# Feed-forward of a tree-routed audio block: ACT weighs four of eight levels, GpSimd adds the residual, and the four groups of an overflow tile are added up in one PSUM bank

## What is computed

```python
for _ in range(DEPTH + 1):                      # 8 levels of a binary tree with 255 nodes
    score = einsum('td,td->t', x, w1s[current]) + b1s[current]
    choice = ((sign(score) + 1) / 2)
    current = current * 2 + choice + 1
path_weights = gelu(abs(logits), approximate=False)       # (2992 tokens, 8)
for i in range(DEPTH + 1):
    t_i = einsum('td,tdo->to', x, w2s[nodes_i]) + b2s[nodes_i]    # a 64x64 matrix of the token's own node
    out = out + t_i * path_weights[:, i][:, None]
return h + out
```

## Time and profile before

| | us |
|---|---|
| median of 3 runs | 495.93 (495.58 to 497.63) |
| the profiled execution, its own time | 497.14 |
| its span (first to last instruction) | 495.4 |
| from the first product of the feed-forward (365.07) to the span's end | 130.3 |

### The profile page before, as it was taken

How to read it: one execution, slowest core, us unless ns; L and a number is a source line. 1 busy time by engine, 2 the same in 40 slices (tenths; PEclk the granted TensorE clock), 3 DMA queues, 4 the chain that set the end, 5 groups by cost and what they waited for, 6 DMA issues and landing times.

```text
span 495.4 us, 8210 instructions
## 1 busy us (share of the span) xinstructions
PE 362.6 (73%) x2578; PEld 246.1 (50%) x2578; DVE 353.8 (71%) x619; ACT 297.0 (60%) x691; POOL 266.6 (54%) x354
## 2 busy tenths in 40 slices
PE   1158997767998897878987798834069887778880
PEld 1145665545555554456644475522057665545550
DVE  0558869897988888988889979776129999433341
ACT  1357987799789986777976658561013332544551
POOL 4324687885686846855896617417506555321111
PEclk9988989999999999898998989855569999999997
DMA  4443541339969722312441200197151220000000
GB/s 95 120 104 84 125 101 41 93 78 226 202 146 156 162 53 63 93 33 63 110 109 27 69 1 11 38 133 99 32 132 35 56 54 10 6 7 4 7 3 7
DMA packets 58424, 36.99 MB, mean 75 GB/s; under 512 B 31645, under 2 KB 57079, under 8 KB 58378
## 3 DMA queue, kind: packets, MB, share of 16 engines
q1 hardware_dynamic: 54250, 33.55, 33.6%
q0 software_dynamic: 3328, 2.36, 1.9%
q10 hardware_dynamic: 800, 0.49, 0.5%
HBM read 11.15 MB, written 7.50 MB: 38 GB/s over the span
## 4 chain that ended last, share of the span: by engine, by line
DVE 39%; PE 27%; ACT 15%; issue 11%; DMA 5%; POOL 1%; SPq 1%; DVEq 0%; POOLq 0%; ACTq 0%
DVE nm L1367 12%; ACT Z L1183 8%; PE Z L914 8%; DVE pre L1634 6%; PE Z L1051 5%; DVE va L1626 4%; DMA pre<-in_x 3%; DVE va L1396 2%; PE Z L1053 2%; ACT q L1125 2%; PE Z L1057 2%; DVE pre L1463 1%; ACT k L1125 1%; ACT va L1276 1%; PE Z L1055 1%
## 5 line engine op out<-in xcount | busy, mean ns | idle before, releaser
L1367 DVE TENSOR_REDUCE nm<-Z 125x1 f32<-125x748 f32 x192 | 175.4, 932 | 38.9 <-PE Z L914 33.2
L1183 ACT ACTIVATE Z<-Z,nm 125x748 f32<-125x748 f32 x192 | 166.1, 870 | 61.5 <-DVE nm L1367 61.2
L914 PE MATMUL Z<-pool_a 128*125 128x512 f16 (+1 forms) x768 | 164.5, 342 | 27.3 <-ACT Z L1183 23.7
L914 PEld LDWEIGHTS Z<-pool_a 128*125 128x125 f16 x768 | 88.7, 141 | 71.6 <-ACT Z L1183 45.6
L717 POOL DMA_INDIRECT out<-pre,va x44 | 42.7, 971 | 87.8 <-DVE pre L1640 78.3
L1634 DVE TENSOR_REDUCE pre<-va 128x64 f32<-128x512 f32 x44 | 45.1, 1025 | 1.3
L1276 ACT COPY va<-Z 32x520 f32<-32x520 f32 x48 | 27.9, 580 | 30.3 <-PE Z L1057 30.1
L781 PE MATMUL Z<-xhT,wq 128*128 128x249 f16 (+1 forms) x192 | 33.4, 295 | 10.5 <-DVEq L1377 9.2
L1183 ACT ACTIVATION_READ_ACCUMULATOR Z<-Z,nm 125x1 f32 x192 | 41.1, 214 | 0.0
L1051 PE MATMUL Z<-pool_a,qk 128*32 x96 | 29.6, 390 | 14.1 <-ACT va L1276 8.7
L646 POOL DMA_INDIRECT sorted_rows<-xrow,slot x24 | 30.4, 1266 | 15.3 <-DVE slot L1519 8.7
(11 more groups left out here) (237 smaller groups left out, 620.9 us busy)
## 6 DMA issues: line engine op xcount, KB each, us to landing
pool_a<-pool_a SPq DMA_DIRECT2D x64, 187.0 KB, 3.3
pool_a<-pool_a SPq DMA_DIRECT2D x64, 93.5 KB, 2.2
sorted_rows<-zrow SPq DMA_DIRECT2D x1, 3640.0 KB, 22.1
va<-sorted_rows SPq DMA_DIRECT2D x11, 260.0 KB, 3.4
w<-in_L_ffn_w2s SPq DMA_DIRECT2D x1, 2048.0 KB, 16.6
pre<-in_x SPq DMA_DIRECT2D x4, 375.0 KB
pool_a<-in_L_ffn_w2s SPq DMA_DIRECT2D x1, 1024.0 KB
out<-pre,va POOLq DMA_INDIRECT x44, 2.1
```

Of the source, the lines that this page charges most:

```text
L914: last = mm(z[0:XP, c0:c1], kst[:, u % 3, a, hd, KST[t]:KST[t] + XP], qst[:, u % 3, hd, c0:c1], start=(a == 0), stop=(a == 1))
L1183: sc_.activation(z, z, ACT.Exp, bias=nm[0:XP, u % 4, i:i + 1], accum_out=sm[0:XP, u % 4, i:i + 1]).then_inc(s_exp, 1)
L1367: v.tensor_reduce(nm[0:XP, u % 4, i:i + 1], Z[n % 3][0:XP, 0:N], X, ALU.max, negate=True).then_inc(s_max, 1)
```

## The change

Four edits in the feed-forward:

1. ACT weighs the first four levels of each tile (`weigh_first`: four ACTIVATE of 128x64 from PSUM, scaled by a column of `gw`), DVE the other four.
2. GpSimd adds the residual in `rows_out`, ahead of the tile's output DMA; `add_residual` is gone.
3. An overflow tile uses one bank pair like a static one. Each group is multiplied with all 128 columns of weights, 32 of them with the group's rows and 96 zero, and the four groups are added up in the bank. For that ACT spreads the transposed rows in `xm`, where each group's 32 columns stand between blocks of zeros that are written once (`apart_zeros`). The four copies to `yv` are gone.
4. The leaves of four groups lie in one number (`lam4`, two more DVE operations before `group_offsets`). PE loads one number for a tile, after group 0 of the tile before; each node is `(leaves >> (7 * g + sh)) & mask`. The load for a block's first tile now stands ahead of the block's `If`.

```diff
             def rows_out(k):
+                pool.wait_ge(s_sl, k + 1)
+                o = yo[:, k % NO, :]
+                gp.tensor_tensor(o, o, xs[:, (k // 4) % NX, k % 4, C_H:C_ID], ALU.add).then_inc(s_yo, 1)
                 pool.wait_ge(s_yo, k + 1)
...
             def bank_ready(n):
-                if n >= ST_TILES + NY:
-                    pe.wait_ge(s_yv, n - NY - ST_TILES + 1)
-                elif n >= NY:
+                if n >= NY:
                     pe.wait_ge(s_wy, n - NY + 1)
+                    pe.wait_ge(s_wa, n - NY + 1)
...
                 def node(g, sh):
-                    if g % 2:
-                        return pairs[g // 2] >> (7 + sh)
-                    return (pairs[g // 2] >> sh) & (LEAVES - 1 >> sh)
+                    return (leaves >> (7 * g + sh)) & (LEAVES - 1 >> sh)
                 tile_ready(k)
-                xk = xsT[:, k // 4 % 3, (k % 4) * P:(k % 4 + 1) * P]
+                bank_ready(k)
+                y = y_bank(k)
                 for g in range(4):
-                    if g == 2 and k % 4 < 3:
-                        following = load_leaves(k + 1)
-                    bank_ready(banks(k) + g)
-                    y = Z[1 + (banks(k) + g) % NY][0:G, :]
-                    xg = xk[:, G * g:G * (g + 1)]
-                    mm(y[:, 0:4 * E1], xg, wlow[:, bass.ds(node(g, 4) * (4 * E1) + T03 * E1, 4 * E1)], start=True, stop=True)
+                    xg = xm[:, k // 4 % 2, k % 4, P * g:P * (g + 1)]
+                    f, l = g == 0, g == 3
+                    mm(y[:, 0], xg, wlow[:, bass.ds(node(g, 4) * (4 * E1) + T03 * E1, 4 * E1)], start=f, stop=l)
...                                                        (three more products, alike)
+                    if g == 0 and k % 4 < 3:
+                        following = load_leaves(k + 1)
...
             for m in range(ST_TILES // 4, F_TILES // 4):
+                leaves = load_leaves(4 * m)
                 with pe.If(groups > 4 * (4 * m - ST_TILES)):
                     xs_T(m)
-                    pairs = load_leaves(4 * m)
...
+            def weigh_first(k):
+                act.wait_ge(s_gelu, k + 1)
+                if k >= 2:
+                    act.wait_ge(s_sl, k - 1)
+                y = y_bank(k)
+                for n in range(AW):                                  # AW = 4
+                    last = sc_.activation(wy[:, k % 2, n * D:(n + 1) * D], y[:, 0, n, 0:D], ACT.Copy,
+                                          scale=gw[:, k % 4, n:n + 1])
+                last.then_inc(s_wa, 1)
...
                     for k in range(4 * m, 4 * m + 4):
-                        if k >= ST_TILES + 2:
-                            act.wait_ge(s_wy, k - 1)
-                        for g in range(4):
-                            act.wait_ge(s_y, banks(k) + g + 1)
-                            sc_.copy(yv[g * G:(g + 1) * G, k % 2], y_bank(banks(k) + g)[0:G]).then_inc(s_yv, 1)
-                        act.wait_ge(s_yv, 4 * (k - ST_TILES + 1))
-                        gates(k, yv[:, k % 2])
+                        gates(k)
+                        weigh_first(k)
...
             def weigh(k):
-                v.tensor_tensor(wy[:, k % 2].rearrange("p (h l o) -> p h l o", h=2, o=D), y[:, :, :, 0:D],
-                                gw[:, k % 4].rearrange(...).to_broadcast([P, 2, 4, D]), ALU.mult).then_inc(s_wy, 1)
+                v.tensor_tensor(w[:, 1], y[:, 1, :, 0:D], gv[:, 1], ALU.mult).then_inc(s_wy, 1)
             def sum_levels(k):
                 dve.wait_ge(s_wy, k + 1)
+                dve.wait_ge(s_wa, k + 1)
```

More of the change, by code:

```diff
@@ L1029, in load_leaves, with overflow_products @@
                 kk = k - ST_TILES
-                return [nc.tensor.value_load(lami[0:1, 2 * kk + i:2 * kk + i + 1], min_val=0,
-                                             max_val=LEAVES * LEAVES - 1) for i in range(2)]
-            def overflow_products(k, pairs):
+                return nc.tensor.value_load(lam4[0:1, kk:kk + 1], min_val=0, max_val=LEAVES ** 4 - 1)
+            def overflow_products(k, leaves):
                 following = None
                 def node(g, sh):
-                    if g % 2:
-                        return pairs[g // 2] >> (7 + sh)
-                    return (pairs[g // 2] >> sh) & (LEAVES - 1 >> sh)
+                    return (leaves >> (7 * g + sh)) & (LEAVES - 1 >> sh)
@@ L1059, in overflow_products @@
+                last.then_inc(s_y, 1)
                 return following
@@ L1242, in _, with apart_zeros @@
             sc_.activation(warm[:], half[0:1, 0:1], ACT.Gelu)
+            def apart_zeros():
+                act.wait_ge(*freed["sl", B - 1])
+                n = 8 * 4 * (P + G)
+                sc_.copy(pre[:, NO * D:NO * D + n], zrow[:, 0:1].to_broadcast([P, n])).then_inc(s_xmz, 1)
             def xs_copy(m):
@@ L1246, in xs_copy, with xs_copy_apart, gates @@
                 if m >= 3:
-                    act.wait_ge(s_y, banks(4 * (m - 2)))
+                    act.wait_ge(s_y, 4 * (m - 2))
                 sc_.copy(xsT[0:D + 1, m % 3, :], Z[0][0:D + 1, 512 * (m % 2):512 * (m % 2) + 512]).then_inc(s_xc, 1)
-            def gates(k, y):
+            def xs_copy_apart(m):
+                act.wait_ge(s_xp, m + 1)
+                if m >= ST_TILES // 4 + 2:
+                    act.wait_ge(s_y, 4 * (m - 1))
+                sc_.copy(xm[0:D + 1, m % 2].rearrange("p t (g c) -> p t g c", c=P + G)[:, :, :, 0:G],
+                         Z[0][0:D + 1, 512 * (m % 2):512 * (m % 2) + 512].rearrange(
+                             "p (t g c) -> p t g c", t=4, g=4)).then_inc(s_xc, 1)
+            def gates(k):
+                act.wait_ge(s_y, k + 1)
                 if k >= 4:
                     act.wait_ge(s_wy, k - 3)
+                y = y_bank(k)
                 w = gw[:, k % 4].rearrange("p (h l) -> p h l", h=2)
@@ L1262, in _ @@
                     xs_copy(k // 4 + 1)
-                act.wait_ge(s_y, k + 1)
-                gates(k, y_bank(k))
+                gates(k)
+                weigh_first(k)
             act.wait_ge(s_goff, 1)
@@ L1268, in _ @@
                 with act.If(groups > 4 * (4 * m - ST_TILES)):
-                    xs_copy(m)
+                    xs_copy_apart(m)
                     for k in range(4 * m, 4 * m + 4):
-                        if k >= ST_TILES + 2:
-                            act.wait_ge(s_wy, k - 1)
-                        for g in range(4):
-                            act.wait_ge(s_y, banks(k) + g + 1)
-                            sc_.copy(yv[g * G:(g + 1) * G, k % 2], y_bank(banks(k) + g)[0:G]).then_inc(s_yv, 1)
-                        act.wait_ge(s_yv, 4 * (k - ST_TILES + 1))
-                        gates(k, yv[:, k % 2])
+                        gates(k)
+                        weigh_first(k)
         @block.vector
```

46 lines of the change are left out of this document (18 added, 28 removed).

## The result

The kernel after takes **511.01 us** (median of 4 runs, 510.44 to 511.34), the kernel before on the same chip 496.78 (4 runs, 495.58 to 504.49): ratio 1.029, 95% interval 1.026 to 1.033. It is slower. The forecast was 507.2, range 500 to 512. On the span it is 508.5 against 495.4, so +13.1 where the sum said +11.3.

A forecast was written before the change was run, and what follows sets the result against it. The prediction took DVE to bound the static tiles and PE's instruction stream the overflow tiles. Static -4.0, between stages +1.5, overflow addresses +11.7 and end +2.1 gave +11.3 on the 495.9 us median: 507.2 us, range 500 to 512.

The forecast's parts named there:

- Ahead of the feed-forward: Before the first feed-forward product, near 365 us: the little work added there is covered, so 0 change.
- Static tiles: PE's 29 steps between static tiles go from 1.64 to 1.50 us: -4.0 us.
- the bound of -4.9: Largest gain allowed for the static stage, with PE at its own need of 1.47 us a tile.
- the ring of 12: Static stage: GpSimd falls ten output tiles behind DVE, twelve buffers just cover it with 1.3 us to spare; cost 0.
- The 239 ns: ACT's weighings: skill-page spacing at 64 columns, giving 1.53 us a tile and ACT as bound; the profile row was preferred.
- Between the stages and in the overflow: Block-opening copies queue behind weighings, +1.5 us; longer node addresses in PE's instruction stream, +11.7 over three blocks.
- The end: Behind the last product: three skipped blocks each load leaves ahead of their If, +2.1 us if PE's stream ends the span.
- The sum: Whole span: -4.0 + 1.5 + 11.7 + 2.1 = +11.3 us on 495.4, so a median of 507.2.
- Rival A: Overflow groups: register work hides, the array's 1.10 us a group decides, blocks 20.1 us, whole 488 to 490.5; chance 0.11.
- B: Whole kernel balances: longer addresses cost half, the end nothing; +3.3 us or less, 494 to 498.4; chance 0.07.
- C: Static stage: GpSimd's step of 2.4 us or more fills the output ring, stopping DVE, then PE; 509 to 512; chance 0.14.

The follow-up runs named there:

- static_edits_alone: Kernel before plus ACT's weighing of four levels and GpSimd's residual addition, overflow tiles unchanged but for that addition: 494.9 us, ratio 0.992 to before.
- copies_one_leaf: Kernel before plus both static edits, one packed load a tile, each group's leaf taken out once, PE's Ifs nested; four banks and copies stay: 484.1 us, ratio 0.963.
- dve_weighs_eight: Kernel after with DVE weighing all eight levels again, GpSimd still adding the residual: 511.0 us, one run; static tile 1.637 us.
- ring_of_eight: Kernel after with a ring of 8 output tiles instead of 12: 517.3 us, ratio 1.036 to the kernel before.
- nested_skip: Kernel after with PE's Ifs nested, so one jump passes all three unused blocks: 507.8 us, one run.
- one_leaf_value: Kernel after with each group's leaf taken out of the packed number once and the load inside the If: 488.5 us, ratio 0.984 to before.
- load_in_if: Kernel after with the load for a block's first tile moved back inside the If, behind the transposes: 510.4 us, ratio 1.023 to before.

## Why the prediction was right, point by point

**Ahead of the feed-forward: 0 forecast, +4.0 measured.** This is the step that failed: "all four edits lie behind 365 us, so only the last 130 us count". A time was given for the whole kernel, and the part that the diff leaves alone was not constant. Some 1.1 us have come by 26 us, where GpSimd's subtraction in the split of the input (L502) takes 1.79 us and 1.08 in the kernel before, with the same DVE work beside it in both; about 2 between 275 and 290, where the granted clock is lower (windows, before and then after, 260 to 292):

```profile
260.00:292.00 32.00, 25.44 (x142) 16.83 (x141) 27.38 (x54) 19.96 (x46) 15.96 (x24) 0.89 0.15 37
```

```profile
260.00:292.00 32.00, 26.94 (x133) 17.49 (x133) 25.68 (x52) 18.68 (x43) 17.06 (x26) 0.79 0.19 45
```

The last 0.8 lie behind the last exponential (L1183 before).

The same code moved by 3.3 us between two executions, so 4.0 can be of that kind. At the last exponential the other profiles stand between 1.2 us earlier and 6.5 later than before's first, in steps of 1 to 3 us that come at other places from one profile to the next. It doesn't take ACT's zeros: static_edits_alone and copies_one_leaf don't write them and have their first product at 367.1 and 369.9. Whether a part of the 4.0 belongs to the new kernel's code stays open, since before stood at 365.1 twice and eight of the ten profiles with the new overflow lie at 366 to 372.

**Static tiles: -4.0 forecast, -6.0 measured.** The term was mis-sized: I took 1.50 us for three engines near each other, and PE holds its own need, 1.455, without a loss to the others. The measured -5.3 of tiles 2 to 31 is even beyond the bound of -4.9, because that need was put at 1.47: the transposes stand in six of the 29 steps and not in every fourth, and the step behind them is 1.27. The first two tiles, which I had left out, gave 0.7 more. dve_weighs_eight and ring_of_eight show that the reasons were right: halving DVE's weighing is what frees PE, and the ring of 12 just covers GpSimd. That edit 2 is needed beside it is shown only for the kernel as built: without it the late signals take the gain away, not DVE's cycle of 1.40. ACT's four weighings start 0.20 us apart (0.93 for four). The 239 ns that the prediction works out from the Trainium skill (ScalarE: Activation LUTs, "What ACT_TABLE_LOAD costs") for a following ACTIVATE were not seen here; the row's 0.20 was the nearer guide, as the prediction had it.

**Between the stages and in the overflow: +13.2 forecast, +13.0 measured.** Two small errors cancel: the copy for the first block comes 0.2 us later and not 0.9, and the three blocks take 0.5 more than said. The stream's pace of 0.33 us for shift and mask holds for all four products of a group, and a block is 25.9 us, the figure given. The kernels nested_skip and ring_of_eight had 13.7 and 17.7 us at half clock in this stage and the same blocks to 0.1 us (25.90 and 26.05; 25.93 and 26.09); a stage that the array sets grows, as the first block of one_leaf_value did by 1.26 us for 3.4. one_leaf_value against load_in_if, where the register work alone differs, shows the cause: blocks of 26.0 us fall to 20.5. A load of leaves takes 0.65 where I had 0.71.

**The end: +2.1 forecast, +2.14 measured,** but by load_in_if the mechanism is not shown; the agreement to 0.04 us is in part luck, as the branches took 11.0 to 12.3 us from one profile to the next and 13.6 in load_in_if. What is shown is that PE's branches over empty blocks take 3 to 5 us each and end behind GpSimd, and that nesting the Ifs gives back what exceeds GpSimd's 10.6 us (in the profiles; nested_skip has one run).

**The sum.** -2.0 in the static stage, +4.0 ahead of it and -0.2 in the rest take the sum from +11.3 to the +13.1 of the spans: two errors of opposite sign. The median is 3.8 us above the forecast, 0.75%: 1.8 of it are these, 1.2 the step from the profiled time of before down to its median, which the kernel after did not need (its profiled execution took 510.76, its median is 511.01), and the rest what lies around the span, 2.3 us where before had 1.7. Rival A would have needed one line more in the change; B is out, as the longer address cost the whole of what I took; C's mechanism is real, but decides with a ring of 8 and not with 12.

## What to carry to other kernels

Where products have addresses from registers, read the starts of the weight loads: a spacing that doesn't follow the size of the product is PE's instruction stream, and then the number of register instructions for each address is the cost. Take a packed field out once and derive the rest by single shifts; here that alone was worth 22 us (load_in_if to one_leaf_value), more than the 15 that the four edits together moved. An engine freed of work gains only what the next one leaves (1.64 to 1.455, PE's own need), and an addition moved off a DMA-issuing engine may change the pace of its DMAs. A time for a whole kernel has the spread of the untouched part in it: compare stage by stage, from a mark inside the kernel.

## What the runs showed that I had not expected

- An overflow stage set by PE's stream absorbs half clock: with 6.8, 10.2, 13.7 and 17.7 us of it (load_in_if, after, nested_skip, ring_of_eight) the three blocks took 76.7, 76.9, 76.7 and 76.8 us. A group takes 2.1 us while it lasts, but the groups behind it come at 1.11 and not at the stream's 1.34, until the array has caught up.
- PE's branch over an empty block of four tiles took 2.8 to 5.2 us, while the queue that loads instructions moved packets of 16 KB; the same three branches took 11.8 us before, 11.9 after and 13.6 in load_in_if.
- With output DMAs 1.45 us apart, updates of semaphores by products came up to 3.7 and 3.5 us after the product's end in the two executions of that kernel, and in none of the twelve other profiles did ACT, when free, wait over 1.5 us for one; the cause is open.
